# Cross-attention over a long context: raw turned context from memory, norm folded into key weights, division moved to the output stage

## The reference

```python
ctx = _layernorm(context, ln_g, ln_b)
q = x @ Wq                                   # x is layer-normed before
k, v = jnp.split(ctx @ Wkv, 2, axis=-1)      # 16 heads of 64 each
sim = jnp.einsum('bhid,bhjd->bhij', q, k) * scale
attn = jax.nn.softmax(sim, axis=-1)
out = jnp.einsum('bhij,bhjd->bhid', attn, v)
return out.transpose(0, 2, 1, 3).reshape(B, Nq, INNER) @ Wo
```

## Time and profile before

| what | value |
|---|---|
| median of 3 runs | 2017.91 us (2017.11 to 2163.83) |
| profiled execution, its own time | 2020.24 us |
| its span, first to last instruction | 2018.5 us |
| mean granted TensorE clock (share of full) | 0.961 |
| busy: PE, DVE, ACT, POOL | 91%, 79%, 61%, 28% |
| first score matmul of the attention stage | 115.65 us |
| DMA, mean | 85 GB/s |

### The profile page before, as it was taken

The page is one execution under the profiler, slowest core; times in us unless marked ns, Lnnn a source line. Parts: engine busy times, 40 slices in busy tenths (PEclk is TensorE's granted clock), DMA queues, the critical chain, the costliest instruction groups (busy, mean ns, idle before and its releaser), DMA issues. The chain is left out here.

```text
span 2018.5 us, 33904 instructions
## 1 busy us (share of the span) xinstructions
PE 1843.3 (91%) x10010; PEld 1513.9 (75%) x10010; DVE 1601.7 (79%) x2790; ACT 1225.7 (61%) x2259; POOL 559.9 (28%) x388
## 2 busy tenths in 40 slices
PE   5978999999999999999999999999698756999995
PEld 4757777777777777777777777777485446999994
DVE  6758888898798988988889889878574856888863
ACT  3436666666676666766766767666452425777751
POOL 3022423334234232342342423412003731000003
PEclk9989999999999999999999999999798977999996
DMA  4621111111111111111111111010552026666632
GB/s 157 269 74 36 40 49 56 40 40 47 53 47 38 38 57 48 43 42 58 45 38 40 55 48 46 22 32 11 197 199 99 1 100 214 210 214 204 219 119 73
DMA packets 158260, 172.49 MB, mean 85 GB/s; under 512 B 13528, under 2 KB 124912, under 8 KB 158192
## 3 DMA queue, kind: packets, MB, share of 16 engines
q1 hardware_dynamic: 156656, 167.44, 25.6%
q0 software_dynamic: 1536, 4.20, 0.6%
HBM read 127.04 MB, written 44.56 MB: 85 GB/s over the span
## 5 line engine op out<-in xcount | busy, mean ns | idle before, releaser
L590 POOL TENSOR_TENSOR cl<-nrm,ch 128x255 fp32r<-128x255 f32 (+1 forms) x208 | 308.8, 1487 | 577.0 <-DVE ch L762 577.0
L688 ACT ACTIVATE s<-score 128x512 f32<-128x512 f32 (+1 forms) x416 | 248.4, 597 | 352.2 <-PE score L127 352.1
L721 DVE TENSOR_TENSOR s<-s,most 128x512 f32<-128x512 f32 (+1 forms) x416 | 321.9, 774 | 69.4 <-ACT most L664 69.4
L727 DVE TENSOR_TENSOR pl<-s,ph 128x512 fp32r<-128x512 f32 (+1 forms) x416 | 357.7, 860 | 0.7 <-ACT ph L670 0.7
L125 PE MATMUL acc<-ph,cl 128*128 128x512 f32 (+1 forms) x832 | 342.3, 411 | 1.4 <-DVE pl L727 1.4
L125 PE MATMUL score<-qsh,tl 128*128 128x512 f32 (+1 forms) x832 | 339.0, 407 | 0.8 <-DVE tl L756 0.8
L127 PE MATMUL score<-qsh,th 128*128 128x512 f32 (+1 forms) x832 | 326.7, 393 | 0.0
L126 PE MATMUL score<-qsl,th 128*128 128x512 f32 (+1 forms) x832 | 326.6, 393 | 0.0
L127 PE MATMUL acc<-ph,ch 128*128 128x512 f32 (+1 forms) x832 | 326.0, 392 | 0.0
L126 PE MATMUL acc<-pl,ch 128*128 128x512 f32 (+1 forms) x832 | 325.6, 391 | 0.0
L739 DVE TENSOR_TENSOR top<-top,s 128x512 f32<-128x512 f32 (+1 forms) x352 | 250.2, 711 | 19.4 <-ACT s L688 19.3
(11 more groups left out here) (257 smaller groups left out, 3456.6 us busy)
## 6 DMA issues: line engine op xcount, KB each, us to landing
raw<-in_ctx_in SPq DMA_DIRECT2D x192, 128.0 KB, 2.0
wr<-in_W SPq DMA_DIRECT2D x45, 512.0 KB, 4.8
queries_scratch<-stage SPq DMA_DIRECT2D x32, 512.0 KB, 3.5
qr<-queries_scratch SPq DMA_DIRECT2D x64, 256.0 KB, 3.3
outputs_scratch<-o SPq DMA_DIRECT2D x64, 256.0 KB, 2.4
at<-outputs_scratch SPq DMA_DIRECT2D x16, 1024.0 KB, 7.6
wr<-in_Wg SPq DMA_DIRECT2D x15, 1024.0 KB, 7.1
wr<-in_Wl SPq DMA_DIRECT2D x15, 1024.0 KB, 5.7
```

The source lines that it names most:

```text
L590: pool.tensor_tensor(cl[0:rows(t), t, 1:DIM], nrm[0:rows(t), t, 1:DIM], ch[0:rows(t), t, 1:DIM].bitcast(F32), ALU.subtract).then_inc(r_low, 1)
L688: act.activation(s[0:n, u, t, :], score[0:n, slot(0, u, t) % 2, :], ACT.Copy).then_inc(copied, 1)
L721: v.tensor_tensor(s[0:n, u, t, :], s[0:n, u, t, :], most[0:n, u, :], ALU.subtract).then_inc(shifted, 1)
L727: v.tensor_tensor(pl[0:n, ring(t), :], s[0:n, u, t, :], ph[0:n, ring(t), :].bitcast(F32), ALU.subtract).then_inc(p_low, 1)
```

## The change: what it does

1. **Scores from raw, turned context.** The host hands over the context a second time with rows and columns exchanged. SP loads it four tiles at once (`load_turned`; 52 groups of up to 512 KB in all, the last of a batch one tile of 65) to a new buffer `turned`. `th` and `tl` are made from it; the transposes on TensorE go.
2. **The norm.** VectorE multiplies the key weights `wk` by the gain and takes each row's mean off, ahead of splitting them, in `queries`; a product and a difference of 128 x 2048 elements, a reduction over them, and the small division of its result. The copies to `stage` no longer scale. The inverse deviation of a context row is now the scale of ScalarE's copy of the scores (`rnow`, copied once a batch). The row tiles `nrm` are made as before.
3. **Sums.** In `attend` the sums, their turning, reciprocal, spreading and the products `o<-acc,inv` go. ScalarE copies `acc` (2 x 512 columns) to `o` once a unit. In `project_out` the sums are read back from memory, inverted at once, stored, loaded in another form (`ir`), spread by two matmuls for each half (`pi`), copied by ScalarE (`iv`), and VectorE multiplies `pv` by them (`vu`) before the split. `at` holds three halves instead of four.
4. **The maximum** is subtracted from PSUM (`misc`, now two banks) with no copy to `most`.
5. **Low parts** `cl` and `qsl` move from GpSimd to VectorE; GpSimd keeps the inverse root.

```diff
@@ queries @@
             def _(sp):
                 sp.dma_start(wq[:, :, :], Wq.rearrange("(c p) n -> p c n", p=P)).then_inc(wq_in, 16)
+                sp.dma_start(wk[:, :, :], WkT.rearrange("(j p) d -> p j d", p=P)).then_inc(wk_in, 16)
+                sp.dma_start(gain_row[:, :], g_row.rearrange("(a d) -> a d", a=1).broadcast_to([P, DIM])
+                             ).then_inc(row_in, 16)
+                for t in range(KT):
+                    cx.load(sp, ctx_in, 0, t, raw_in)
+                for g in range(GROUPS):
+                    cx.load_turned(sp, turned_in, turned_last, 0, g, turned0[g])
...
             def _(v):
                 ln.vector_normalise(v, x_in)
+                v.wait_ge(wk_in, 16)
+                v.wait_ge(row_in, 16)
+                v.tensor_tensor(wk[:, :, :], wk[:, :, :], gain_row[:, :].unsqueeze(1).broadcast_to([P, PAIRS, DIM]),
+                                ALU.mult).then_inc(wk_scaled, 1)
+                v.wait_ge(wk_scaled, 1)
+                v.tensor_reduce(wk_sum[:, :], wk[:, :, :], AX_X, ALU.add).then_inc(wk_summed, 1)
+                v.wait_ge(wk_summed, 1)
+                v.tensor_scalar(wk_mean[:, :], wk_sum[:, :], 1.0 / DIM, None, ALU.mult).then_inc(wk_meaned, 1)
+                v.wait_ge(wk_meaned, 1)
+                v.tensor_tensor(wk[:, :, :], wk[:, :, :], wk_mean[:, :].unsqueeze(2).broadcast_to([P, PAIRS, DIM]),
+                                ALU.subtract).then_inc(wk_centred, 1)
                 ln.vector_split(v)
@@ attend @@
+                    for n, g in later(k.groups(at_turned)):
+                        wait(sp, t_low, tile(n - 1, min(TG * (g + 1), KT)))
+                        cx.load_turned(sp, turned_in, turned_last, n, g, turned_arrived[g])
...
-                        pool.tensor_tensor(ql[:, u], qr[:, :, :], qh[:, u].bitcast(F32), ALU.subtract
-                                           ).then_inc(q_low, 1)
-                    for n, t in k.context(at_rows):
-                        pool.wait_ge(r_high, tile(n, t) + 1)
-                        pool.tensor_tensor(cl[0:rows(t), t, 1:DIM], nrm[0:rows(t), t, 1:DIM],
-                                           ch[0:rows(t), t, 1:DIM].bitcast(F32), ALU.subtract).then_inc(r_low, 1)
...
-                    for n, t in k.context(at_turn):
-                        wait(pe, c_norm, tile(n - 1, t) + 1)
-                        wait(pe, t_low, tile(n, t))
-                        for c in range(DC):
-                            m = pe.transpose(turn[:, c, 0:rows(t)], nrm[0:rows(t), t, c * P:(c + 1) * P],
-                                             ident[0:rows(t), 0:rows(t)])
-                        m.then_inc(c_turn, 1)
...
-                        act.activation(s[0:n, u, t, :], score[0:n, slot(0, u, t) % 2, :], ACT.Copy
-                                       ).then_inc(copied, 1)
+                        act.activation(s[0:n, u, t, :], score[0:n, slot(0, u, t) % 2, :], ACT.Copy,
+                                       scale=rnow[0:n, t:t + 1]).then_inc(copied, 1)
...
-                        act.activation(sums[0:1, :], acc[0:1, u, 0, :], ACT.Copy).then_inc(sum_row, 1)
+                        act.activation(o[:, u], acc[:, u], ACT.Copy).then_inc(drained, 1)
...
-                        v.tensor_tensor(s[0:n, u, t, :], s[0:n, u, t, :], most[0:n, u, :], ALU.subtract
+                        v.tensor_tensor(s[0:n, u, t, :], s[0:n, u, t, :], misc[0:n, u], ALU.subtract
...
+                    if (f := k.unit(-4)):
+                        r, u = f
+                        v.wait_ge(q_high, unit(r, u) + 1)
+                        v.tensor_tensor(ql[:, u], qr[:, :, :], qh[:, u].bitcast(F32), ALU.subtract).then_inc(q_low, 1)
...
+                    for n, t in k.context(at_rows_low):
+                        m = rows(t)
+                        v.wait_ge(r_high, tile(n, t) + 1)
+                        v.tensor_tensor(cl[0:m, t, 1:DIM], nrm[0:m, t, 1:DIM], ch[0:m, t, 1:DIM].bitcast(F32),
+                                        ALU.subtract).then_inc(r_low, 1)
@@ project_out @@
+                    if p == 1:
+                        sp.wait_ge(inverted, 1)
+                        sp.dma_start(IV.rearrange("k b n -> (k b) n"), parts_of_one[:, :]).then_inc(parts_out, 16)
+                        sp.wait_ge(parts_out, 16)
+                        sp.wait_ge(whose_made, 1)
+                        for hh in range(2):
+                            sp.dma_start(ir[hh * PAIRS:(hh + 1) * PAIRS, :].rearrange("k (b t) -> k b t", t=NQ),
+                                         IV[:, :, hh * NQ:(hh + 1) * NQ]).then_inc(parts_in, 16)
...
+                        pe.matmul(pi[:, t, :], whose_r[:, p, :], irl[:, cols], start=True, stop=False)
+                        pe.matmul(pi[:, t, :], whose_r[:, p, :], irh[:, cols], start=False, stop=True
+                                  ).then_inc(i_made, 1)
...
-                        act.wait_ge(v_made, 2 * p + t + 1)
+                        act.wait_ge(i_made, 2 * p + t + 1)
+                        wait(act, v_scaled, 2 * p + t)
+                        act.activation(iv[:, :], pi[:, t, :], ACT.Copy).then_inc(i_copied, 1)
+                        act.wait_ge(v_scaled, 2 * p + t + 1)
...
+                        v.wait_ge(i_copied, 2 * p + t + 1)
+                        v.wait_ge(v_made, 2 * p + t + 1)
+                        wait(v, v_low, 2 * p + t)
+                        v.tensor_tensor(vu[:, :], pv[:, t, :], iv[:, :], ALU.mult).then_inc(v_scaled, 1)
```

More of the change, by code:

```diff
@@ L346, in _ @@
                         copy_q(p + 1)
-                    take(act, lambda o, i, g: act.activation(o, i, ACT.Copy, scale=g), p, 0, k_act)
+                    take(act, lambda o, i: act.activation(o, i, ACT.Copy), p, 0, k_act)
             @block.vector
@@ L431, in batch, with groups @@
         return [n] if c % SLOTS == 0 and (not isinstance(n, int) or 0 <= n < B) else []
+    def groups(self, at):
+        found = []
+        for g in range(GROUPS):
+            c = self.c - at(g)
+            if c % SLOTS == 0:
+                n = self.r + c // SLOTS
+                if not isinstance(n, int) or 0 <= n < B:
+                    found.append((n, g))
+        return found
     def context(self, at):
@@ L492, in attend @@
         top = sb("top", [P, UQ], F32)
-        top_col_s, inv_col_s = sb("top_col_s", [P, 4], F32), sb("inv_col_s", [P, 4], F32)
-        sums = sb("sums", [1, UQ], F32)
-        most = sb("most", [P, 2, UQ], F32)
-        inv = sb("inv", [P, UQ], F32)
+        top_col_s = sb("top_col_s", [P, 4], F32)
+        turned, rnow = cx.turned, sb("rnow", [P, KT], F32)
         o = sb("o", [P, 2, DC, UQ], F32)
@@ L499, in attend @@
         acc = ps("acc", [P, 2, DC, UQ])
-        turn = ps("turn", [P, DC, P])
-        misc = ps("misc", [P, 4, P])
+        misc = ps("misc", [P, 2, 4, P])
         raw_in = [sem(f"raw_in{t}") for t in range(KT)]
+        turned_arrived = [sem(f"turned_in{g}") for g in range(GROUPS)]
+        rated = sem("rated")
         q_in = sem("q_in")
@@ L525, in attend @@
         at_root = -14
-        at_rows = spread(LAG - KT + 1)
+        at_rows, at_rows_low = spread(LAG - KT + 1), spread(LAG - KT + 2)
         def later(found):
             return [f for f in found if not (isinstance(f[0], int) and f[0] == 0)]
-        def along_partitions(pe, column, done):
-            for q in range(4):
-                m = pe.transpose(misc[:, q, :], column[:, q:q + 1].broadcast_to([P, P]), ident[:, :])
-            m.then_inc(done, 1)
         with nc.Block() as block:
@@ L621, in step @@
                         if t == 0:
-                            wait(pe, scaled, DC * (unit(r, u) - 1))
+                            wait(pe, drained, unit(r, u) - 1)
                         if u == 0:
@@ L659, in step @@
                 def step(k):
-                    if (f := k.unit(KT + 4)):
-                        r, u = f
-                        act.wait_ge(top_spread, unit(r, u) + 1)
-                        wait(act, shifted, KT * (unit(r, u) - 1))
-                        act.activation(most[:, u, :], misc[:, :, :], ACT.Copy).then_inc(top_row, 1)
+                    for n in k.batch(0):
+                        if not isinstance(n, int) or n > 0:
+                            act.wait_ge(c_shift, n)
+                        wait(act, copied, SLOTS * n)
+                        act.activation(rnow[:, :], rstd[:, :], ACT.Copy).then_inc(rated, 1)
                     if (f := k.back(LAG - 2)):
@@ L687, in step @@
                         wait(act, p_low, slot(r - 1, u, t) + 1)
-                        act.activation(s[0:n, u, t, :], score[0:n, slot(0, u, t) % 2, :], ACT.Copy
-                                       ).then_inc(copied, 1)
-                    for n, t in k.context(at_turn):
-                        act.wait_ge(c_turn, tile(n, t) + 1)
+                        if u == 0 and t == 0:
+                            act.wait_ge(rated, r + 1)
```

(10 more changed lines are left out.)

188 lines of the change are left out of this document (108 added, 80 removed).

## The result

The changed kernel takes 1899.74 us (median of four runs, 1897.99 to 1907.26). In the same comparison the kernel before has a median of 2019.25 over four runs, one of which, at 2163.83, is a slow one; the other three have a median of 2017.91, and the ratio goes by them: 0.941, with a 95% interval of 0.938 to 0.944. The prediction had 1906 against 2017.9.

What follows compares the result with a forecast made beforehand. TensorE was taken to bound the attention stage, VectorE having slack. The terms -131.0 + 2.7 - 5.7 - 3.5 + 5.0 + 21 = -111.5 us, from a median of 2017.9, gave 1906 us, range 1885 to 1968.

Steps and rivals of the forecast that it cites:

- TensorE's starts set the pace: Attention stage: TensorE bounds it; removing 8.19 us of its work a batch takes 131.0 us off, pace 72.7 us.
- VectorE keeps up: Attention stage: VectorE has 67.6 us of work in a 72.7 us batch, 93%, so no cost is charged.
- the loop in the output stage: Output stage: `vu`, `vh`, `ath`, `atl` wait in turn, 10.8 us a pair; pairs 1 to 5 cost 12.3 us.
- The 2.7 us that I gave back for the tiles turned ahead of the first score: Attention stage: seven first-batch tiles were already turned before the first score, so 7 x 0.38 us of saving comes back.
- the first rival: Attention stage: VectorE's waits at the maxima stay, a batch takes 77.1 us, the kernel 1976; wholly or in part 0.14.
- The slower rival: Attention stage: stretching of `pl` and `s` and the waits both stay; 84.7 us a batch, kernel 2096; chance 0.04.
- the stretching: Attention stage: GpSimd lengthens VectorE's `pl` and `s`; moving the low parts removes 7.6 us a batch of VectorE's time.
- ScalarE: Attention stage: it ends at 63 of 72.7 us a batch, is no bound, and nothing is charged.
- Entry and exit: Around the attention stage: first score comes 5.7 us sooner after its query load, and the end is 3.5 us shorter.
- Projection of the queries: Ahead of the attention stage: VectorE's four new operations, 7.1 us, make the projection 5.0 us later.
- Output stage: End of the attention layer: 21 us later in all, 12.3 from the loop and 8 to 9 from the start.
- the rival at half clock: Output stage: TensorE falls to 1.2 GHz, eight pairs take 148 us against 88, kernel 1966; chance 0.08.

Runs made afterwards that it cites:

- a2: Changed kernel with two idle transposes of the identity put back on TensorE for each context tile; 1947.71 us, 0.963 of the kernel before.
- a3: Changed kernel with TensorE's two groups for the sums and the spread of their inverses put back as idle work; 1952.75 us, 0.967 of the kernel before.
- b2: Changed kernel with one more unread subtraction on VectorE for every `cl`; 1906.56 us, 0.944 of the kernel before.
- a1: Changed kernel with the low parts `cl` and `qsl` made on GpSimd again; 1907.78 us, 0.944 of the kernel before.
- c1: Changed kernel with GpSimd's low parts in the query projection moved to VectorE, GpSimd keeping zero fillings and root; 1893.50 us, 0.937 of the kernel before.
- a4: Changed kernel with VectorE's `atl` put off behind the next half's `vu` in the output stage; 1896.20 us, 0.939 of the kernel before.
- b3: Kernel before with only the low parts `cl` and `qsl` moved to VectorE; 2028.07 us, 1.005 of the kernel before.
- b1: Changed kernel with GpSimd's `wql` in the projection held until VectorE has normalised x; 1899.92 us, 0.940 of the kernel before.
- b5: Changed kernel with three more unread subtractions on VectorE for every `cl`, each waiting for the one before; 2103.11 us, 1.041 of the kernel before.

## Why the prediction was right

The median lies 6 us (0.3%) under the forecast, inside its range. The mechanisms held: TensorE's starts set the pace, VectorE keeps up, the loop in the output stage binds. That the sum is so close is in part luck. The attention stage saved 9 us more than forecast, the projection and the output stage cost 3 us more, and within the output stage two errors of 5 to 6 us cancel.

**TensorE's starts set the pace: right.** 312 starts and the groups for the maximum make 72.73 us; 72.87 was measured, and a2 and a3 show that the work taken off TensorE is paid in full when it is put back. The saving was set too small by 9.3 us. The larger part is one reading: the earlier trace rows take an interval of 73.4 us in, which is shorter than the steady ones, so 80.92 stood for a steady 81.47; that is 0.55 a batch, 8.8 in all. The pace after was 0.14 slower than forecast, which takes 2.2 of it back. The 2.7 us that I gave back for the tiles turned ahead of the first score don't appear: 16 x 8.60 is 137.6, the whole difference.

**VectorE keeps up: right.** 66.8 us of work a batch against 67.6 forecast, 5.8 of waits against 5.1, `pl` at 682. b2 took two thirds of this slack and cost 3 us, which refutes the first rival, whose waits at the maxima were to stay. The slower rival is refuted by `pl` itself. It was right too that the stretching is GpSimd's doing. It did not matter for the pace, though: a1 has it back, at an equal pace, and VectorE's work there is even a little less, 804.78 / 900 x 72.88 = 65.2 us a batch.

What the rows show of the maximum in PSUM: `s` takes 678 ns with one input from there, `pl` 682 with both from SBUF. The Trainium skill (VectorE: DVE Perf Modes, the section on the TRN2 errata) has a longer fixed time for an operand in PSUM, 120 cycles against 58; an estimate by that page would have `s` some 65 ns longer than `pl`. The trace doesn't agree with it.

**ScalarE: right, with a smaller load than counted.** 706.37 / 900 x 72.87 = 57.2 us a batch against 63: the scale for each partition brings a copy of 512 to 689 ns, 0.09 more than the 0.60 of a plain one, near the lower end of the "nothing to 0.3". The 0.3 had no row behind it; the kernel before had such a copy, `stage` with `gain` in the projection, at 0.69 us.

**Entry and exit: right,** -5.3 and -3.3 against -5.7 and -3.5.

**Projection of the queries: too small, +9.0 instead of +5.0 at the first key product.** I moved VectorE's steps back by the four new operations and kept their durations. But the steps moved against GpSimd's. Before, both `ln_hTl` were all but over, at 1.2 us each, when GpSimd began its `wkl`; now the second one meets it and takes 5.44, 4.2 more. VectorE wins some of that back, since its own `wkl`, which now begins after GpSimd's is over, takes 2.29 instead of 4.83, but then waits 1.33 for `qf`; the first `ql` ends at 40.96, where the forecast had 38. And it is no longer `ql` alone that decides: TensorE waited for the second `ln_hTl` too, begins the second half of its projections at 35.41, and comes to the first key product at 42.11, 1.15 us behind `ql`. Its starts are 0.42 us apart in that stretch up to 40.7, where they are 0.23 behind it. c1, without GpSimd's arithmetic, has both `ln_hTl` at 1.2 and a first key product at 34.25. By the load of the queries 1.9 of the 9.0 are made up again; no run takes apart where.

**Output stage: the loop right, the sum by luck.** A half takes 5.40 us against 5.4, and a4 shows by what. But the +22.3 against +21 is made up otherwise than forecast. The start was to cost 8 to 9. Up to the `vh` that opens the first pair it is 29.6 us after the first matmul instead of 23.8, and the first pair takes 17.5 instead of 8.6: 14.7 together. In that pair two `atl` (1335.20 to 1342.36) take 7.16 us beside GpSimd's `wol` (1333.45 to 1338.01) instead of twice 2.29. The kernel before had the same, at 7.18, but there no `vh` waited for VectorE; now the next `vu` stands behind them. The five pairs with the loop cost 11.0 instead of 12.3 (1398.17 - 1343.00 against 1511.54 - 1467.33), and the pair behind them, in which no `atl` is made any more, gives 3.4 back, which the forecast did not count. The granted clock stayed at 0.88, so the rival at half clock did not come about. The start of the stage, with the inverses stored and loaded again, was not tried apart.

## What to carry to other kernels

Take the pace between markers from the steady part of the loop, not from the first to the last marker; here that alone was 9 us. When a step is moved on one engine, look at what runs beside it on the other engine at its new place, since its duration is a property of the place as well. Split a stage's difference before you call its forecast right: in the output stage two errors cancelled. And shorter operations on an engine that does not set the pace gain nothing by themselves: b3 made VectorE's operations shorter, and the kernel took half a per cent longer.

## What the runs showed of the hardware

**Where GpSimd began first, VectorE is held until GpSimd's operation ends, not slowed in part.** In the changed kernel `wkl` on GpSimd ends at 34.27 and `ln_hTl`, begun at 29.91, ends 1.08 later, which is about the 1.22 us that it takes alone. In b1 `wql` ends at 17.84 and the product of the key weights ends 2.15 later (2.28 alone). GpSimd's filling of `wkl`, which follows from 17.78 to 21.29, does not hold that product. Not all operations are held: TENSOR_REDUCE of b1, with one input, begins within the same filling and takes its 2.29, but the small TENSOR_SCALAR `ln_ve` of c1, also with one tensor input, takes 1.78 instead of 0.17 and ends with the filling. The Trainium skill (GPSIMD Engine Reference, the section Key points) names VectorE's instructions "in a 2-port perf mode or with two SBUF inputs"; the rows fit this for the second kind, and for the scalings if those run in such a mode, which no run here shows.

**The same program comes out either way, by when two loads land.** In a1, whose projection is that of the changed kernel, `ln_xn` took 2.67 us. GpSimd's `wql`, which waits for `wq`, began at 12.38 there, when the scalings were nearly through (9.95 + 2.67 = 12.62), and at 11.72 in the changed kernel, where it caught them earlier and they took 7.6 us more. Eight profiles have this projection: in six `wql` began 1.6 to 2.1 us after the first scaling, and the eight took 10.3 us; in two (a1 and b5) it began 2.3 and 2.4 after it, and they took 2.7.

```profile
9.95 2.67 DVE L91 TENSOR_SCALAR ln_xn<-res_x,ln_mv,ln_rstd 128x256 f32<-128x256 f32 x8 [1.80 <-POOL ln_rstd L96]
...
12.38 4.61 POOL L290 TENSOR_TENSOR wql<-wq,wqh 128x2048 fp32r<-128x2048 f32 x1 [2.47 <-ACT wqh L348]
```

So the first key product was seen at 37.8 (a1) and 39.1 (b5), and at 41.1 to 43.7 in the other six. A difference of 5 us between two profiles of such a kernel needn't come from the edit.
